# Weighted sums of gathered rows: from VectorE multiply-adds to TensorE products with diagonal matrices

## The chip, the cores and the metric

## The reference, cut to what matters

`x` has 2048 rows of 128 values. Four blocks follow each other, each added to `x` after a layer norm: a graph attention in hyperbolic space over a 2048x2048 mask, a linear layer computed in logarithms, a second graph attention, and a causal attention with 8 heads whose keys and values are looked up in a product-key memory. Only the last is touched:

```python
q = (x @ Wq).reshape(b, n, HEADS, DIM) * DIM ** (-0.5)
kv_scores, indices = _pk(x, Wq_pk, pk_keys)          # 16 best rows and their softmax weights
ind = indices + offsets[None, None, :, None]
k = jnp.einsum('bnhk,bnhkd->bnhd', kv_scores, keys_table[ind])
v = jnp.einsum('bnhk,bnhkd->bnhd', kv_scores, values_table[ind])
sim = jnp.einsum('bihd,bjhd->bhij', q, k)
...
attn = jax.nn.softmax(sim, axis=-1)
out = jnp.einsum('bhij,bjhd->bhid', attn, v)
```

For each of the 2048 positions and each head, 16 rows of 256 values (key and value side by side in one table) are fetched and summed with 16 weights. `_pk` finds the 16 best of 128x128 key pairs: the top 16 of each of two lists of 128 similarities, then the top 16 of the sums, of which 54 can qualify.

## The kernel before, in words

The positions are cut in T = 16 tiles of 128, one position per partition. Each engine has an instruction stream of its own, written out by hand, and the streams meet only at semaphores. The first 300 us or so hold the three earlier blocks. The last block then runs 8 heads x 16 tiles. Head 0 is written out, heads 1 to 6 are a hardware loop, head 7 is written out.

The gather (GpSimd, L281 to L291). For each tile GpSimd waits for the 16 row numbers of each position (`rows_full`) and for a free ring slot (`slot_free`), then issues 16 indirect DMAs, one for each k, each fetching 128 rows of 1 KB into `ring[:, t % 4, k, :]`. The ring has 4 slots, so the gathers run up to four tiles ahead. Semaphores `gathered[slot][quarter]` tell of each 4 landed DMAs; the last one of a head has `last_in`.

VectorE's step (L809 to L898). In step t it finds the row numbers of tile a = t + 4 (`find_start` to `find_best_second`, `find_best_index`, `look_up_1` to `look_up_5`), normalises the weights of tile t + 3 (`weigh_1`, `weigh_2`), takes the maximum over the scores of tile t - 1 (`score_max`), adds the finished output of tile t - 2 into `xs` (`add_out_1`, `add_out_2`), and, between all these, computes the 16 weighted sums of tile t: `sum_rows(t, k)` is acc = ring * weight + acc over 128x256, with `acc` in PSUM and the last one writing `kv[:, t, :]` (L749 to L755). The small operations are laid between the sums so that a result is never read by the next instruction. After the last sum the slot is given back (L882).

TensorE's step (L1639 to L1656). `project(t + 5)`: queries and the similarities with the product keys, with a wait for ScalarE between. `exponentials()`: wait for the softmax of tile t - 1. `values(t - 1)`: the probabilities are transposed in groups of four blocks, copied by ScalarE, multiplied with the values, then projected by `wo`. `turn_keys(t)`: wait for `kv_full`, transpose the new keys. `scores(t)`: q times all keys up to tile t, so that the work grows with t.

ScalarE's step (L1307 to L1322) holds the copies out of PSUM and the exponentials that go with these: `exp_best`, `project_out`, `softmax(t - 1)`, `turned_out(t - 1)`, `key_out(t)`.

The start of the last block overlaps with the end of the second graph attention: `masked(1, t)` on VectorE prepares its rows, and the searches for tiles 0 to 4 and the two halves of tile 0's sums (`sum_half`, L906) are laid between these and the closing ELU and normalisation of each group of tiles (`elu_in`, `elu_out`, `normal`, L957 to L971), which ScalarE (L1260 to L1267) and TensorE (L1549 to L1555) follow.

## Time and profile before

| | |
|---|---|
| runs | 2860.98, 2866.45, 2868.05 us; median 2866.45 |
| profiled execution | span 2859.2 us; the profile gives no other time of it |
| busy | PE 56%, PEld 43%, DVE 83%, ACT 26%, POOL 69% |
| DMA | 291.44 MB, mean 102 GB/s |
| mean granted TensorE clock | 0.702 |

The span runs from the first to the last instruction of the profiled execution, so it is a little shorter than a device time. PE is TensorE's matmuls, PEld its weight loads, DVE is VectorE, ACT ScalarE, POOL GpSimd. "DVEq", "PEq" and the like are the waits of an engine's instruction queue at a semaphore. Instructions that issue DMAs or handle semaphores aren't counted as busy, the generation of an indirect DMA's descriptors on GpSimd is.

### The profile page before, as it was taken

How to read it: one execution, taken by the hardware profiler on the slowest of the kernel's cores; microseconds unless marked ns; L12 is line 12 of the kernel's file. 1: busy time of each engine (PE TensorE's matmuls, PEld its weight loads, DVE VectorE, ACT ScalarE, POOL GpSimd, SP SyncE). 2: the span in 40 equal slices, each digit the busy share in tenths (PEclk: the TensorE clock that was granted, in tenths of full speed). 3: DMA queues.
4: the chain of work that ended last, by engine and by line, in shares of the span. 5: the costliest groups of instructions: out<-in, count | busy, mean ns of one | idle time of the engine just before them, and what ended most of it. 6: DMA issues, size and time to landing. Idle time of an engine off the chain costs nothing. (4 is left out here: it accounts for less than half of the span.)

```text
span 2859.2 us, 31735 instructions
## 1 busy us (share of the span) xinstructions
PE 1591.0 (56%) x7362; PEld 1220.4 (43%) x7362; DVE 2373.7 (83%) x8263; ACT 744.9 (26%) x1904; POOL 1959.6 (69%) x2064
## 2 busy tenths in 40 slices
PE   6858545664556445554556455554555445554555
PEld 6848434453344334442344234442344333442444
DVE  6689899998888888887888888887888888887874
ACT  5746412231122112221122112221122112221212
POOL 0003777777777777777777777777777777777775
PEclk8969756785578557775677557775678557775678
DMA  4201233333333333333333333333333333333333
GB/s 158 102 1 34 86 103 105 109 107 105 105 108 106 107 105 108 105 106 106 106 108 106 106 105 108 105 107 105 105 108 106 107 105 108 105 107 106 106 105 90
DMA packets 109551, 291.44 MB, mean 102 GB/s; under 512 B 34128, under 2 KB 41808, under 8 KB 107344
## 3 DMA queue, kind: packets, MB, share of 16 engines
q0 software_dynamic: 98304, 268.57, 32.1%
q1 hardware_dynamic: 10080, 20.97, 2.1%
q14 instruction: 127, 1.04, 0.1%
q8 instruction: 32, 0.52, 0.1%
q10 hardware_dynamic: 1008, 0.33, 0.0%
HBM read 288.69 MB, written 1.05 MB: 101 GB/s over the span
## 5 line engine op out<-in xcount | busy, mean ns | idle before, releaser
L288 POOL DMA_INDIRECT ring<-table,rows x2048 | 1952.1, 953 | 714.4 <-issue 587.9
L755 DVE SCALAR_TENSOR_TENSOR ps<-ring,wgt,ps 128x256 f32<-128x256 f32 x1792 | 865.6, 483 | 316.7 <-DMA ring<-table,rows 290.2
L1608 PE MATMUL ps<-ident,work 128*128 128x128 f32 x1088 | 260.2, 399 | 526.7 <-PEq L1601 526.7
L1608 PEld LDWEIGHTS ps<-ident,work 128*128 128x128 f32 x1088 | 201.4, 211 | 581.9 <-issue 581.8
L1622 PE MATMUL ps<-s2w,work 128*128 128x128 f32 x2176 | 418.7, 358 | 35.2 <-PEq L1620 34.4
L1622 PEld LDWEIGHTS ps<-s2w,work 128*128 128x128 f32 x2176 | 381.0, 265 | 84.5 <-issue 82.0
L1590 PE MATMUL ps<-work,qT 128*128 128x512 f32 (+3 forms) x576 | 310.7, 680 | 69.3 <-PEq L1582 64.8
L1296 ACT ACTIVATE s2w<-ps 128x512 f32<-128x512 f32 (+2 forms) x320 | 168.7, 533 | 332.2 <-ACTq L1295 331.8
L1286 ACT ACTIVATE work<-ps,nmax 128x128 f32<-128x128 f32 (+15 forms) x128 | 149.3, 1167 | 318.7 <-ACTq L1284 318.7
L1577 PE MATMUL ps<-ident,work 128*128 128x128 f32 x128 | 46.8, 366 | 316.9 <-PEq L1575 316.9
L1590 PEld LDWEIGHTS ps<-work,qT 128*128 128x128 f32 x576 | 124.9, 238 | 200.0 <-issue 200.0
L761 DVE TENSOR_REDUCE nmax<-ps 128x1 f32<-128x128 f32 (+7 forms) x127 | 160.8, 1266 | 10.8 <-DVEq L760 10.8
L1577 PEld LDWEIGHTS ps<-ident,work 128*128 128x128 f32 x128 | 20.8, 162 | 337.6 <-issue 337.2
L1274 ACT ACTIVATE qpk<-ps 128x128 f32<-128x128 f32 x123 | 34.1, 277 | 491.9 <-ACTq L1273 491.9
L1305 ACT ACTIVATE work<-ps 128x128 f32<-128x128 f32 x128 | 35.4, 277 | 457.1 <-ACTq L1304 457.0
L1571 PE MATMUL ps<-keyd,qpk 128*128 128x256 f32 x246 | 100.5, 496 | 90.3 <-PEq L1570 90.3
L1431 PE MATMUL ps<-work 128*128 128x128 f32 x1024 | 137.8, 280 | 2.8 <-PEq L1428 2.8
L727 DVE TENSOR_TENSOR pick<-bposf,ps 128x864 f32<-128x864 f32 x128 | 134.9, 1054 | 4.4
L731 DVE TENSOR_TENSOR pick<-pick,ps 128x864 f32<-128x864 f32 x128 | 134.9, 1054 | 4.4
L735 DVE TENSOR_REDUCE rowf<-pick 128x16 f32<-128x864 f32 x128 | 134.8, 1053 | 4.4
L1431 PEld LDWEIGHTS ps<-work 128*128 128x128 f32 x1024 | 127.1, 196 | 4.7 <-issue 4.5
L279 POOL TENSOR_TENSOR xs<-xs,bffn 128x512 f32<-128x512 f32 x4 | 5.9, 1477 | 162.6 <-DVE work L341 162.6
(241 smaller groups left out, 2654.3 us busy)
## 6 DMA issues: line engine op xcount, KB each, us to landing
ring<-table,rows POOLq DMA_INDIRECT x2048, 2.7
staged<-adj_in SPq DMA_DIRECT2D x16, 1024.0 KB, 4.8
xs<-x_in SPq DMA_DIRECT2D x4, 256.0 KB, 6.3
wpkq<-w_pkq SPq DMA_DIRECT2D x8, 128.0 KB
out<-xs SPq DMA_DIRECT2D x1, 832.0 KB, 4.4
keyd<-pk_keys SPq DMA_DIRECT2D x16, 32.0 KB
wo<-w_o SPq DMA_DIRECT2D x8, 64.0 KB
out<-xs SPq DMA_DIRECT2D x1, 192.0 KB, 2.1
```

Of the source, the lines that this page charges most:

```text
L288: nc.gpsimd.indirect_dma_start(ring[:, t % RING, k, :], None, table_d, bass.IndirectOffsetOnAxis(ap=rows[:, t % RING, k:k + 1], axis=0),). ...
L727: v.tensor_tensor(pick[:, :, :], bposf[:, :].unsqueeze(2).to_broadcast([P, TOPK, NCAND]), iota_ps.unsqueeze(1).to_broadcast([P, TOPK, NCAN ...
L731: v.tensor_tensor(pick[:, :, :], pick[:, :, :], cand_ps.unsqueeze(1).to_broadcast([P, TOPK, NCAND]), ALU.mult).then_inc(dve_done, c.one())
L735: v.tensor_reduce(rowf[:, :], pick[:, :, :], X, ALU.add).then_inc(dve_done, c.one())
L755: return v.scalar_tensor_tensor(out, row, w, acc_ps, ALU.mult, ALU.add)
L761: v.reduce_max(nmax[:, t % 2:t % 2 + 1], ps[:, 4:8, :].rearrange("p b n -> p (b n)")[:, 0:(t + 1) * P], X, negate=True).then_inc(nmax_full, 1)
L1286: s.activation(prob[:, t % 2, 0:L], ps[:, 4:8, :].rearrange("p b n -> p (b n)")[:, 0:L], ACT.Exp, bias=nmax[:, t % 2:t % 2 + 1], accum_out ...
L1296: s.activation(pts[:, (parity + b) % 2, 0:n * P], ps[:, 2 + (parity + b) % 2, 0:n * P], ACT.Copy).then_inc(pt_sb, 1)
L1431: ins = m.matmul(ps[:, OUT_BANKS[layer][t % banks], 0:D], ptg[:, n % 3, i * P:(i + 1) * P], hB[:, j, :], start=(j == 0), stop=(j == T - 1))
L1590: ins = m.matmul(ps[:, 4 + at // 512, 0:w], qT[:, t % 8, :], kT[:, at:at + w], start=True, stop=True)
L1608: ins = m.transpose(ps[:, 2 + (parity + b) % 2, j % 4 * P:(j % 4 + 1) * P], prob[:, t % 2, j * P:(j + 1) * P], ident[:, :])
L1622: ins = m.matmul(ps[:, 1, 0:P], kv[:, j, D:2 * D], pts[:, (parity + b) % 2, j % 4 * P:(j % 4 + 1) * P], start=(j == 0), stop=(j == t))
```

## The change

VectorE no longer sums. For each tile it makes one product, `spread(t)`: the 128x128 identity (a copy of it in PSUM) times each of the tile's 16 weights, 16 diagonal matrices side by side, 128x2048 elements, into one of two buffers that held rows of the graph attention. TensorE multiplies each diagonal matrix with the gathered rows of that k and accumulates the 16 products in PSUM (`sums`); ScalarE waits for that, gives the slot back, and copies the sum to `kv` (`kv_out`). The waits for landed rows move from VectorE to TensorE. The sums of tile t stand in TensorE's step ahead of the values of tile t - 1. In the last tile of the last head they are split around these. VectorE's step loses the interleaving; its parts follow each other with full fences (`drain`) between. The row numbers get 8 slots instead of 4. In the start, the search for tile 4 moves ahead of the ELU and normalisation of the last groups, and the sums of tile 0 are TensorE's and ScalarE's, ahead of their part of those groups.

```diff
-        rows = sb("rows", [P, RING, TOPK], U32)
+        rows = sb("rows", [P, ROWS, TOPK], U32)
...
+        kv_ps, end_ps = ps[:, 1, 2 * D:4 * D], ps[:, 0, 0:2 * D]
+        ident_ps = ps[:, 0, 3 * D:4 * D]
+        def diag(t):
+            return stagedf[:, 1 + t % 2, :].rearrange("p (k n) -> p k n", k=TOPK)
...
-            def sum_rows(t, k):
-
-                row, w = ring[:, t % RING, k, :], wgt[:, t % 4, k:k + 1]
-                if k == 0:
-                    return v.tensor_scalar(acc_ps, row, w, None, ALU.mult)
-                out = acc_ps if k < TOPK - 1 else kv[:, t, :] if t > 0 else acc[:, 0, :]
-                return v.scalar_tensor_tensor(out, row, w, acc_ps, ALU.mult, ALU.add)
+            def spread(t):
+
+                v.tensor_tensor(diag(t), ident_ps.unsqueeze(1).to_broadcast([P, TOPK, P]),
+                                wgt[:, t % 4, :].unsqueeze(2).to_broadcast([P, TOPK, P]), ALU.mult).then_inc(diag_ready, 1)
```

VectorE's step after the change:

```python
if find: find_start(a)
if out: add_out_1((t - 2) % T)
v.drain()
if find: find_replace(a)
if out: add_out_2((t - 2) % T)
v.drain()
if find: find_second(a)
if begun: score_max((t - 1) % T)
if not (last and t == T - 1): spread((t + 1) % T)
v.drain()
if find: find_index(a)
if weigh: weigh_1((t + AHEAD - 1) % T)
v.drain()
if weigh: weigh_2((t + AHEAD - 1) % T)
if find: find_all(a)
```

The start on VectorE, behind `find_all(3)`:

```diff
-            elu_out(3)
-            sum_half(0, 0)
-            normal(3)
-            elu_in(4)
-            weigh(2)
-            elu_out(4)
-            sum_half(0, 1)
-            normal(4)
-            rows_done(1)
-            find_halves(4)
-            find_all(4)
...
+            spread(0)
+            weigh(2)
+            find_halves(4)
+            elu_out(3)
+            find_all(4)
+            normal(3)
+            elu_in(4)
+            elu_out(4)
+            normal(4)
```

ScalarE and TensorE:

```diff
+            def kv_out(t, of=kv_ps):
+
+                act.wait_ge(sum_full, 1)
+                act.sem_inc(sum_full, -1)
+                act.sem_inc(slot_free, 1)
+                s.activation(kv[:, t, :], of, ACT.Copy).then_inc(kv_full, 1)
...
             query_out()
             sim_out(AHEAD)
+            kv_out(0)
...
+            def sums(h, t, quarters, to=kv_ps):
+
+                for q in quarters:
+                    if q == 0:
+                        pe.wait_ge(diag_ready, 1)
+                        pe.sem_inc(diag_ready, -1)
+                    landed(h, t, q)
+                    for k in range(q * QK, (q + 1) * QK):
+                        if t == T - 1 and k == TOPK - 1:
+                            pe.wait_ge(last_in, h * 16 + 16)
+                        ins = m.matmul(to, diag(t)[:, k, :], ring[:, t % RING, k, :], start=(k == 0), stop=(k == TOPK - 1))
+                    if q == QUARTERS - 1:
+                        ins.then_inc(sum_full, 1)
```

TensorE's step after the change, without its first step:

```python
project((t + AHEAD + 1) % T)          # not in the last head's last tiles
if last and t == T - 1:
    sums(h, t, (0,), end_ps)
    exponentials()
    past_scores(t).then_inc(s_full, 1)
    sums(h, t, (1, 2), end_ps)
    values(t - 1, PARITY[t - 1], bank1, t)      # quarter 3, key turn and own scores in its middle
    return
if t == 0:
    exponentials()
    values(T - 1, PARITY[T - 1], bank1)
    bank1()
    sums(h, 0, range(QUARTERS))
    kv_copied()
else:
    if t > 1:
        bank1()
    sums(h, t, range(QUARTERS))
    exponentials()
    values(t - 1, PARITY[t - 1], kv_copied)
turn_keys(t)
scores(t)
```

## Rows read from the trace of the kernel before

**Rows 1.** Page, first part: busy us (share of span) xinstructions.
```profile
PE 1591.0 (56%) x7362; PEld 1220.4 (43%) x7362; DVE 2373.7 (83%) x8263; ACT 744.9 (26%) x1904; POOL 1959.6 (69%) x2064
```

**Rows 2.** Line L288: ns min/median/max, first to last start; idle us, times.
```profile
L288 POOL DMA_INDIRECT ring<-table,rows x2048: 942/946/2361, 254.4 to 2836.4; - x187
...
  POOLq L286: 125.6, 115
```

**Rows 3.** GpSimd timeline: start us, us, operation, [idle before <-releaser].
```profile
308.93 1.14 POOL L288 DMA_INDIRECT ring<-table,rows  x1 [1.55 <-POOLq L286]
310.38 2.36 POOL L288 DMA_INDIRECT ring<-table,rows  x1 [0.30 <-issue]
...
357.33 0.94 POOL L288 DMA_INDIRECT ring<-table,rows  x1 [6.43 <-POOLq L286]
...
1401.19 0.95 POOL L288 DMA_INDIRECT ring<-table,rows  x1 [0.30 <-issue]
...
2836.43 0.95 POOL L288 DMA_INDIRECT ring<-table,rows  x1 [0.30 <-issue]
```

**Rows 4.** Groups by line, 600:2700: xcount | busy, mean ns | idle before.
```profile
L755 DVE SCALAR_TENSOR_TENSOR ps<-ring,wgt,ps 128x256 f32<-128x256 f32 x1482 | 715.1, 482 | 279.8 <-DMA ring<-table,rows 259.1
...
L727 DVE TENSOR_TENSOR pick<-bposf,ps 128x864 f32<-128x864 f32 x105 | 110.7, 1054 | 3.6
```

**Rows 5.** VectorE's timeline in the start, 300 to 357.
```profile
309.63 2.29 DVE L470 CUSTOM_DVE_ANT_0 staged<-staged,ring 128x2048 f32<-128x2048 f32 x1
...
326.78 0.40 DVE L738 CAST rows<-rowf 128x16 uint32<-128x16 f32 x1
...
334.18 0.16 DVE L565 TENSOR_TENSOR sc<-sc 128x4 f32<-128x4 f32 x1 [0.17 <-DVEq L310]
...
346.95 0.29 DVE L675 MAX8 half<-sim 128x8 f32<-128x128 f32 x1 [0.17 <-DVEq L673]
...
356.25 0.17 DVE L738 CAST rows<-rowf 128x16 uint32<-128x16 f32 x1
```

**Rows 6.** ScalarE's timeline in the start, 348 to 353.
```profile
348.86 0.38 ACT L1197 ACTIVATE aT<-ps 128x256 f32<-128x256 f32 x1 [1.08 <-ACTq L1196]
...
352.76 0.38 ACT L1280 ACTIVATE sim<-ps 128x256 f32<-128x256 f32 x1 [1.46 <-ACTq L1277]
```

**Rows 7.** TensorE timeline: an early light step, then a heavy one.
```profile
377.06 1.19 PE L1571 MATMUL ps<-keyd,qpk 128*128 128x256 f32 x2 [0.71 <-PEq L1570]
...
1565.08 3.46 PE L1590 MATMUL ps<-work,qT 128*128 128x512 f32 x8 [0.54 <-PEq L1582]
...
1578.02 1.94 PE L1608 MATMUL ps<-ident,work 128*128 128x128 f32 x8 [7.21 <-PEq L1601]
...
1586.18 0.46 PE L1637 MATMUL ps<-wo,oT 128*128 128x128 f32 x2 [0.54 <-PEq L1636]
...
1588.04 0.67 PE L1571 MATMUL ps<-keyd,qpk 128*128 128x256 f32 x2 [0.71 <-PEq L1570]
```

**Rows 8.** Windows: length, busy by engine, granted clock, DMA share, GB/s.
```profile
50.00:100.00 50.00, 50.00 (x442) 49.93 (x441) 40.48 (x66) 39.85 (x59) 0.00 (x0) 0.98 0.54 193
400.00:2780.00 2380.00, 1279.55 (x5169) 938.89 (x5170) 2011.69 (x7255) 512.02 (x1384) 1800.20 (x1904) 0.68 0.36 106
```

**Rows 9.** Timelines of VectorE, ScalarE and TensorE at the end, 2820 to 2843.
```profile
2820.85 0.48 DVE L755 SCALAR_TENSOR_TENSOR work<-ring,wgt,ps 128x256 f32<-128x256 f32 x1
2826.14 2.16 DVE L761 TENSOR_REDUCE nmax<-ps 128x1 f32<-128x1920 f32 x1 [4.82 <-DVEq L760]
...
2828.42 1.86 ACT L1286 ACTIVATE work<-ps,nmax 128x1920 f32<-128x1920 f32 x1 [6.25 <-ACTq L1284]
...
2830.52 5.16 PE L1590 MATMUL ps<-work,qT 128*128 128x512 f32 x8 [4.51 <-PEq L1601]
...
2836.97 2.02 PE L1622 MATMUL ps<-s2w,work 128*128 128x128 f32 x16 [0.43 <-PEq L1620]
...
2841.67 0.63 PE L1597 MATMUL ps<-work,qT 128*128 128x128 f32 x2
```

More of the change, by code:

```diff
@@ L675, in find_start @@
                 v.max(half[:, 0, 0, 0:8], sim[:, s, 0:NKEY])
-                v.max(half[:, 1, 0, 0:8], sim[:, s, NKEY:2 * NKEY]).then_inc(dve_done, c.one())
+                v.max(half[:, 1, 0, 0:8], sim[:, s, NKEY:2 * NKEY])
             def find_replace(t):
@@ L775, in add_out_2 @@
                                        ALU.mult, ALU.add).then_inc(bank1_free, 1)
-            def landed(h, t, q):
-                per = [16 * (QK - (q == QUARTERS - 1 and s == T - 1)) for s in range(t % RING, T, RING)]
-                dve.wait_ge(gathered[t % RING][q], h * sum(per) + sum(per[:t // RING + 1]))
-            def sum_even(t, k):
-                sum_rows(t, k).then_inc(dve_done, c.one())
-            def sum_odd(t, k):
-                settle()
-                sum_rows(t, k).then_inc(dve_done, c.one())
-                settle()
             def find_halves(t):
@@ L818, in step @@
                     find_start(a)
-                settle()
-                if last and t == T - 1:
-                    score_max(t - 1)
-                landed(h, t, 0)
-                sum_even(t, 0)
+                if out:
+                    add_out_1((t - 2) % T)
+                v.drain()
                 if find:
@@ L826, in step @@
                 if out:
-                    add_out_1((t - 2) % T)
-                if t == 1:
-                    v.tensor_copy(kv[:, 0, :], acc[:, 0, :]).then_inc(kv_full, 1)
-                sum_odd(t, 1)
-                sum_even(t, 2)
-                if out:
                     add_out_2((t - 2) % T)
+                v.drain()
                 if find:
                     find_second(a)
-                if prev and (t - 1) % T < 8:
+                if begun:
                     score_max((t - 1) % T)
-                sum_odd(t, 3)
@@ L840, in step @@
-                landed(h, t, 1)
-                sum_even(t, 4)
+                if not (last and t == T - 1):
+                    spread((t + 1) % T)
+                v.drain()
                 if find:
                     find_index(a)
-                if prev and (t - 1) % T >= 8 and not (last and t == T - 1):
-                    score_max((t - 1) % T)
-                sum_odd(t, 5)
-                sum_even(t, 6)
-                if find:
-                    find_rows(a)
                 if weigh:
@@ L882, in step @@
[L882 to L897 removed]
+                    find_all(a)
@@ L898, in step @@
+                if last and t == T - 1:
+                    v.drain()
                     dve.sem_inc(out_ready, 1)
@@ L904, in weigh @@
                 weigh_2(t)
-            def sum_half(t, part):
-                for k in range(8 * part, 8 * part + 8):
-                    if k % QK == 0:
-                        landed(0, t, k // QK)
-                    settle()
-                    sum_rows(t, k).then_inc(dve_done, c.one())
-                settle()
-                if part == 1:
-                    dve.sem_inc(slot_free, 1)
             dve.sem_inc(sim_free, 1)
@@ L1291, in turned_out @@
                     if key and b == 2:
+                        kv_out(key, end_ps)
                         key_out(key)
@@ L1317, in step @@
                     return
-                if not (first and t == 0):
-                    softmax((t - 1) % T)
-                    turned_out((t - 1) % T, PARITY[(t - 1) % T])
+                if first and t == 0:
+                    key_out(0)
+                    return
+                softmax((t - 1) % T)
                 if t > 0:
-                    key_out(t)
+                    kv_out(t)
+                turned_out((t - 1) % T, PARITY[(t - 1) % T])
+                if t == 0:
+                    kv_out(0)
+                key_out(t)
             for t in range(T):
@@ L1548, in _, with landed, bank1, kv_copied @@
             operands_ready()
+            def landed(h, t, q):
+                per = [16 * (QK - (q == QUARTERS - 1 and s == T - 1)) for s in range(t % RING, T, RING)]
+                pe.wait_ge(gathered[t % RING][q], h * sum(per) + sum(per[:t // RING + 1]))
+            def bank1():
+                pe.wait_ge(bank1_free, 1)
+                pe.sem_inc(bank1_free, -1)
+            def kv_copied():
+                pe.wait_ge(kv_full, 1)
+                pe.sem_inc(kv_full, -1)
+            def sums(h, t, quarters, to=kv_ps):
[10 more added lines that the diff above has]
+                        ins.then_inc(sum_full, 1)
             attend(1)
@@ L1551, in _ @@
             similar()
+            bank1()
+            sums(0, 0, range(QUARTERS))
             group(3)
@@ L1601, in exponentials, with values @@
                 pe.sem_inc(prob_full, -1)
-            def values(t, parity, key=None):
+            def values(t, parity, bank_free, key=None):
                 last = t // 4
@@ L1624, in values @@
                     if key and b == 1:
+                        sums(HEADS - 1, key, (QUARTERS - 1,), end_ps)
+                        kv_copied()
                         turn_keys(key)
```

143 lines of the change are left out of this document (48 added, 95 removed).

## The prediction, made before the changed kernel was run

> **What bounds the kernel now.** I read the page's busy shares first: VectorE 83%, GpSimd 69%, TensorE 56% [rows 1]. By that alone VectorE looks like the bound, and 1,792 of its instructions are the multiply-adds that this change takes away. The next view says otherwise. The one line of GpSimd that gathers table rows ran 2,048 times, from 254.4 to 2836.4 us, and waited at its semaphore for 125.6 us in all [rows 2]. Its timeline shows where: 83.5 us ahead of the first gather, 1.55 us ahead of gather 33, 6.43 us ahead of gather 65, and then never again more than the 0.30 us that each one has before it [rows 3]. In the steady part a gather is 0.95 us "busy" behind 0.30 us of issue (the one at 1401.19), so one starts each 1.25 us, and the missing 0.30 us is what makes the share look like 69%. From gather 65 at 357.33 to the last at 2836.43 there are 1,983 steps in 2479.1 us, 1.250 us each. So GpSimd issues without a break, and a tile costs 16 x 1.25 = 20.0 us whatever the others do. VectorE's own waits say the same: of the 279.8 us that it idled ahead of its sums between 600 and 2700, 259.1 were for landed rows [rows 4]. The pace is also 1.25 us in the last 57 us, where VectorE has little left to do, so a less busy VectorE doesn't quicken it. The time is then: start up to gather 65 (357.3) + 2479.1 + what follows the last gather (2859.2 - 2836.4 = 22.8). Only the first and the last term can move, unless some engine's work per tile passes 20.0 us.
>
> The profiled execution has a span of 2859.2 us; no time of its own is given beside it. The runs are 2860.98, 2866.45 and 2868.05, so the median is 7.3 us above the span. I work in the span and add 7.3.
>
> **The change, per tile in the steady part.**
> VectorE: out go 16 fused sums of 0.48 us [rows 4], 7.7 us. In comes one product over 128x2048. The trace has no such one; below, it can't be under the 1.05 us that 864 elements take [rows 4], above, three such products of 864 are 3.2 us. One VectorE pass over 128x2048 took 2.29 us [rows 5], and 1.05 x 2048/864 = 2.5; I take 2.3. Fences in place of counted waits cost some 0.04 us each, under 1 us a tile. VectorE falls from 2011.69/119 = 16.9 us a tile [rows 8] to some 12. Worth nothing: it wasn't the bound.
> TensorE: in come 16 products with 256 moving columns. At full clock 1,920 columns took 3.46 us [rows 7], so 256 take 0.43 to 0.46 (a single pair with its latency is 0.67) and 16 take 7.1; at half clock the single pair is 1.19 instead of 0.67 [rows 7], twice the columns' share, and 16 take 13.7 to 14. Weight loads hide, as they do now. TensorE has 1279.55/119 = 10.75 us a tile now, at a mean clock of 0.68 [rows 8]. The sum is 17.9 us with the new products at full clock, 24.8 at half clock; the limit is 20.0. This is the step that decides. In a heavy step: values 8.6 us (1578.02 to 1586.64), past scores 3.46 and 1.1 for key turn and own scores, projection 2.1 (to 1588.71) [rows 7], sums 7.1, together 22.4, of which some 2 come from the slow first microseconds after a 7.21 us idle [rows 7] that the new work would mostly fill. Light steps have some 13. Ring and row buffers let four tiles average out, so I take full or nearly full clock and no stall of GpSimd. Evidence for the clock: where TensorE was busy 50.00 of 50 us it was granted 0.98 [rows 8]; at 54% busy 0.68; and the burst at 1578 begins at half pace and ends at full.
> By the Trainium skill, "TensorE: Matmul & The Clock Gate", section "A second HAM failure mode: psum-queue depth-cycling", short idles between groups can keep the clock going up and down, so that dense-looking work still pays. That speaks against me, and the 0.5 us pauses ahead of many groups here are of that sort; it is rival 1.
> GpSimd: is it slowed by the new wide product? Gather 34 took 2.36 us [rows 3] while VectorE ran a 128x2048 pass with both inputs in SBUF [rows 5]. But the look-up products [rows 4], with one input in PSUM, run beside gathers whose median is 946 ns and least 942 [rows 2], and the new product has its identity in PSUM too. So nothing.
> The Trainium skill, "GPSIMD Engine Reference", section "Specifications", names as contending only VectorE instructions in a two-port mode or with two SBUF inputs; by that rule the sum stays as it is. If it fails here, each tile pays 2.36 - 0.95 = 1.4 us.
> ScalarE: a copy of 128x256, 0.38 us [rows 6], per tile, on an engine that is at 26%. Nothing.
>
> **The start.** GpSimd is through with the fourth tile at 357.33 - 6.43 = 350.9 and waits for the fifth tile's row numbers, written at 356.25 [rows 5]. Now their search is moved ahead. Row numbers of the fourth tile are done at 327.2 [rows 5] (later by 0.6 to 0.8 with the identity copy and the fences, which also move gather 33). Then product 2.3, weights 0.4 (330) and halves 3 (333); halves and search together take 9.5 now, from 346.95 to 356.4 [rows 5], and the search 6.5 of it. The ELU's second part needs an exponential of ScalarE, and a copy of tile 0's sums now stands ahead of it. TensorE can start these sums at 329.4 and needs 7.1 to 14 us; I take 9 (half pace at first): 338.5, copy and exponential to 339.8. ELU part 2.9, search 6.5: 349.3 (347 to 355). Gather 65 goes at 351.2 instead of 357.33: 6.1 us won.
> It is lost at gather 81. The normalisation chain that began at 334.18 [rows 5] now begins at 349.4. It ended at 349.24 [rows 6], 15.06 us later, with 3.8 us in it that were half of tile 0's sums; so now it ends at 360.7. The similarities of tile 5 follow 3.9 us later (349.24 to 353.14 [rows 6]), 364.3 here, and then halves 3.0, score maximum 0.3, product 2.3, weights and second index 1.0, search 6.5: 376.5 to 377.4. Its slot also needs tile 1's sums: first scores until 366, projection 2, sums 7.1 to 14: 375.5 to 382.5, likely 378. Gather 81 started at 357.33 + 20 = 377.33 and now starts at some 378.5 (377.4 to 383). So the start gives -0 to +5, I take +1.5.
>
> **The end.** Now the last-but-one tile's sums finish at 2821.33, its scores' maximum starts at 2826.14 and ends 2828.30, the softmax ends 2830.4 [rows 9]. The values of the tile before, 7.7 us, were done by TensorE while it waited for rows. In the new order TensorE sits in the sums and takes these values after them: the landing's chain is last quarter of sums 1.8, values 7, keys and scores 4.6, maximum 2.3, softmax 2.1, with 0.1 of waits 17.9. Its rows land 20 us ahead of the last tile's, at 2819.3, so 2837.2, against 2830.4. Then, all ahead of the last tile's own scores: past scores 3.5 (5.16 now, at half pace [rows 9]), two quarters of sums 3.6, half of the values 3.5 (2835.5 to 2839.0 now [rows 9]), the last quarter 1.9, ScalarE's copy 0.65, key turn and own scores 2.0: 15.2 together, 2852.4. That is 10.1 us after the 2842.30 at which own scores ended (2841.67 + 0.63 [rows 9]). Bounds: 9 with everything at full clock and overlapped, 20 with sums and values at half pace. From there to the end nothing changes, 17 us. The last rows land at 2839.6, so they are no longer what the end waits for. I take +10.5, for a wait or two more on the way.
>
> **Sum.** 2859.2 + 1.5 + 10.5 = 2871.2 span; + 7.3 = 2878.5, +0.4%.
>
> **Rivals.**
> 1. TensorE becomes the bound, at a clock that stays between. Against: it would be denser than now. For: 10.75 + 14 = 24.8 us at half clock, and in light steps a single pair takes 1.19 us, half pace [rows 7]. If a third of each head's tiles ran at half clock and the buffers took up half of their 4.8 us, 128/3 x 2.4 = +100 us: 2978; at one tile in eight +40 us, 2918. It decides once TensorE's mean passes 20.0 us, at an effective clock under some 0.85 for the sums. 0.14.
> 2. Not slower: the start keeps its 6.1 us because tile 1's sums are at full clock and the fifth search comes sooner than I chain it (VectorE's fences let ELU and search run closer), and the end costs its lower bound of 9. Then -(6.1 - 0.8) + 9 = +3.7: 2870. It decides where gather 81 starts before 374. 0.20.
> 3. The wide product slows the gathers: 128 x 1.4 = +180 us, 2878 + 180 = 3058. Against it stand the look-up products. 0.03.
> 4. It does what it says and the end is also cheaper, since TensorE is warm: 0 or less. A real gain over 0.3% would need more than the 8 us of waits in the start, with a free end: 2857. 0.04.
> The forecast has 0.59.
>
> **Range.** 0.3% of 2866 is 8.6 us, about what can be told from no change: 2857.9 and 2875.1 are the borders. Forecast's own range is 2870 to 2892 (start 0 to 5, end 9 to 20); about a fifth of its chance lies under 2875. Same: 0.59/5 + 0.20 = 0.32. Faster 0.04. Slower 0.64. The range to hold 8 in 10 reaches from rival 2 to the light form of rival 1: 2866 to 2912.
>
> **What would show it.** Right: gathers 1.25 us apart from gather 81 to the last, with no wait over 0.3; gather 65 near 351, gather 81 near 378; VectorE under 65% busy with no change in time; granted clock over 0.85 in the steady part; the last gather near 2838 and 33 us from there to the end instead of 22.8. Wrong: waits of GpSimd for its slots (ScalarE's release after the sums) in the heads, gathers over 0.95 us beside the new product, or a granted clock of 0.5 beside full sums.

## The result: 0.4% slower, and the profile after

The changed kernel takes 2878.88 us (median of 4 runs, 2873.7 to 2882.34). The kernel before, timed beside it on the same chip, takes 2867.16 us (median of 4, 2860.98 to 2868.05). The ratio is 1.0042, with a 95% interval of 1.003 to 1.0053: slower, by 11.7 us. The profiled execution of the changed kernel has a span of 2871.8 us, against 2859.2 before, so the spans differ by 12.6 us and can be used to split the loss. Both profiled executions are 5 to 6 us quicker than their medians, so they are compared with each other and not with these. Every ratio here compares runs of one state, without those more than 1.5% above the fastest of the same kernel, so on some chips it differs from the quotient of the medians beside it.

The code moved by seven lines at the gather: L288 of before is L295 after, its wait L286 is L293. L758 is the new wide product, L1504 are the new products on TensorE, L1141 is ScalarE's copy of the sums.

The page's busy shares and TensorE's granted clock in 40 slices, to be held against [rows 1]:

```profile
PE 2220.4 (77%) x11458; PEld 1784.0 (62%) x11458; DVE 1865.3 (65%) x6336; ACT 779.9 (27%) x2032; POOL 1960.1 (68%) x2064
...
PEclk9969889999899989999999889999999899999999
```

TensorE went from 1591.0 to 2220.4 us busy, VectorE from 2373.7 to 1865.3. 508 us of VectorE's work are gone, and the kernel is not faster. GpSimd's figure is the one that did not move: 1959.6 and 1960.1 us. The gather's line shows the same (ns least/median/most, first to last start, then its waits), to be held against [rows 2]:

```profile
L295 POOL DMA_INDIRECT ring<-table,rows x2048: 940/946/2421, 255.3 to 2839.7; - x187
...
  POOLq L293: 127.3, 109
...
DMA to landing us min/median/max: 2.6/2.8/4.6
```

The same stretch of the steady part as in [rows 8] (length, busy time of PE, PEld, DVE, ACT, POOL, clock, DMA share, GB/s), and the two new groups:

```profile
400.00:2780.00 2380.00, 1868.08 (x9046) 1465.42 (x9044) 1537.72 (x5443) 544.36 (x1506) 1800.05 (x1905) 0.94 0.37 107
```

```profile
L1504 PE MATMUL ps<-ring,staged 128*128 128x256 f32 x4096 | 1019.7, 406 | 229.3 <-DMA ring<-table,rows 209.8
...
L758 DVE TENSOR_TENSOR staged<-ps,wgt 128x2048 f32<-128x2048 f32 x128 | 291.9, 2281 | 0.2 <-issue 0.2
```

Over 119 tiles TensorE has 1868.08/119 = 15.7 us a tile and VectorE 12.9, both under the 20.0 us that GpSimd takes for 16 gathers. The granted clock rose from 0.68 to 0.94. The new products waited 209.8 us for landed rows: TensorE, like VectorE before it, waits for GpSimd. GpSimd's timeline (start us, us, idle before) gives the three parts of the time, to be held against [rows 3]:

```profile
310.53 1.17 POOL L295 DMA_INDIRECT ring<-table,rows  x1 [1.57 <-POOLq L293]
...
352.71 1.03 POOL L295 DMA_INDIRECT ring<-table,rows  x1 [0.30 <-issue]
...
380.93 0.94 POOL L295 DMA_INDIRECT ring<-table,rows  x1 [8.29 <-POOLq L293]
...
2839.72 0.94 POOL L295 DMA_INDIRECT ring<-table,rows  x1 [0.30 <-issue]
```

Gather 65, at 352.71, no longer waits; gather 81 at 380.93 waits 8.29 us, and it did not wait before. From there the 1,967 steps to the last gather take 2458.8 us, 1.250 us each. So the last gather starts at 2839.72 instead of 2836.43, 3.3 us later, and from it to the end of the span are 32.1 us instead of 22.8, 9.3 us more. The two make the 12.6 us.

**The start.** VectorE, ScalarE and TensorE, for [rows 5 to 7]:

```profile
329.03 0.17 DVE L745 CAST rows<-rowf 128x16 uint32<-128x16 f32 x1
329.18 2.29 DVE L758 TENSOR_TENSOR staged<-ps,wgt 128x2048 f32<-128x2048 f32 x1
...
341.42 0.69 DVE L555 SCALAR_TENSOR_TENSOR fin<-fin,work 128x512 f32<-128x512 f32 x1 [6.61 <-DVEq L317]
...
344.27 0.17 DVE L701 CAST half<-pos 128x16 f32<-128x16 uint32 x1
...
350.96 0.20 DVE L745 CAST rows<-rowf 128x16 uint32<-128x16 f32 x1
...
378.71 0.17 DVE L745 CAST rows<-rowf 128x16 uint32<-128x16 f32 x1
```

```profile
340.38 0.38 ACT L1141 ACTIVATE work<-ps 128x256 f32<-128x256 f32 x1 [11.97 <-ACTq L1139]
340.65 0.62 ACT L940 ACTIVATE fin<-fin 128x512 f32<-128x512 f32 x1
...
380.19 0.38 ACT L1141 ACTIVATE work<-ps 128x256 f32<-128x256 f32 x1 [8.69 <-ACTq L1139]
```

```profile
331.61 8.57 PE L1504 MATMUL ps<-ring,staged 128*128 128x256 f32 x32 [3.89 <-PEq L1499]
...
370.44 9.56 PE L1504 MATMUL ps<-ring,staged 128*128 128x256 f32 x32
...
385.07 0.67 PE L1532 MATMUL ps<-keyd,qpk 128*128 128x256 f32 x2 [0.71 <-PEq L1531]
...
400.10 7.07 PE L1504 MATMUL ps<-ring,staged 128*128 128x256 f32 x32
```

The wide product took 2.29 us. TensorE began tile 0's sums after 3.89 us of idleness and took 8.57 us for them, ScalarE's copy stood in its queue from 328.4 until 340.38, and the exponential for the ELU behind it. So the ELU's second part waited 6.61 us of VectorE's time, and the fifth tile's row numbers came at 350.96 to 351.16 instead of 356.42. Gather 81 had its row numbers at 378.88 (the last of VectorE's rows) and then needed the slot of tile 1, whose sums ended at 380.00 after 9.56 us, begun at half pace (the last row shows the same 32 instructions at full clock: 7.07), and whose copy (the one at 380.19) released it.

**The end.** TensorE, with the maximum of the last-but-one tile's scores on VectorE and its softmax on ScalarE, for [rows 9]:

```profile
2822.48 3.47 PE L1504 MATMUL ps<-ring,staged 128*128 128x256 f32 x8 [2.46 <-DMA ring<-table,rows]
...
2836.66 1.89 PE L1504 MATMUL ps<-ring,staged 128*128 128x256 f32 x8
2841.34 3.46 PE L1549 MATMUL ps<-work,qT 128*128 128x512 f32 x8 [2.79 <-PEq L1560]
2844.64 3.62 PE L1504 MATMUL ps<-ring,staged 128*128 128x256 f32 x16
...
2851.41 1.89 PE L1504 MATMUL ps<-ring,staged 128*128 128x256 f32 x8
...
2855.16 0.39 PE L1556 MATMUL ps<-work,qT 128*128 128x128 f32 x2
```

```profile
2836.97 2.16 DVE L765 TENSOR_REDUCE nmax<-ps 128x1 f32<-128x1920 f32 x1 [3.75 <-DVEq L764]
```

```profile
2839.25 1.86 ACT L1214 ACTIVATE work<-ps,nmax 128x1920 f32<-128x1920 f32 x1 [6.26 <-ACTq L1212]
```

The last quarter of that tile's sums ran near half pace (3.47 us for its 8 instructions, against 1.89 for the 8 at 2836.66), then came the earlier tile's values, and the maximum started at 2836.97 where it had started at 2826.14. TensorE idled for 2.79 us until the softmax had ended; only then came past scores, two quarters of the last tile's sums, half of the values and the last quarter, one after another. The last tile's own scores ended at 2855.55, against 2842.30 before.

### The profile page after: what moved, and what is told of

The parts are those of the page before. It is cut to its first block and busy times, and to the rows that moved or that the text cites. A ratio compares the mean times of both kernels' runs of the same rounds, so it can differ in the third digit from the quotient of the medians.

```text
span 2871.8 us, 39679 instructions
## 1 busy us (share of the span) xinstructions
PE 2220.4 (77%) x11458; PEld 1784.0 (62%) x11458; DVE 1865.3 (65%) x6336; ACT 779.9 (27%) x2032; POOL 1960.1 (68%) x2064
## 3 DMA queue, kind: packets, MB, share of 16 engines
HBM read 288.69 MB, written 1.05 MB: 101 GB/s over the span
## 5 line engine op out<-in xcount | busy, mean ns | idle before, releaser
L295 POOL DMA_INDIRECT ring<-table,rows x2048 | 1952.6, 953 | 717.9 <-issue 586.0
L1504 PE MATMUL ps<-ring,staged 128*128 128x256 f32 x4096 | 1019.7, 406 | 229.3 <-DMA ring<-table,rows 209.8
L1504 PEld LDWEIGHTS ps<-ring,staged 128*128 128x128 f32 x4096 | 813.1, 202 | 404.6 <-DMA ring<-table,rows 263.0
L1141 ACT ACTIVATE work<-ps 128x256 f32<-128x256 f32 x128 | 49.0, 383 | 1054.0 <-ACTq L1139 1054.0
L1580 PE MATMUL ps<-s2w,work 128*128 128x128 f32 x2176 | 307.9, 289 | 34.0 <-PEq L1578 33.1
L1580 PEld LDWEIGHTS ps<-s2w,work 128*128 128x128 f32 x2176 | 276.0, 200 | 65.7 <-issue 62.6
L1549 PE MATMUL ps<-work,qT 128*128 128x512 f32 (+3 forms) x576 | 244.2, 554 | 67.6 <-PEq L1541 64.8
L758 DVE TENSOR_TENSOR staged<-ps,wgt 128x2048 f32<-128x2048 f32 x128 | 291.9, 2281 | 0.2 <-issue 0.2
L1567 PE MATMUL ps<-ident,work 128*128 128x128 f32 x1088 | 194.1, 304 | 39.9 <-PEq L1560 21.0
L1549 PEld LDWEIGHTS ps<-work,qT 128*128 128x128 f32 x576 | 102.1, 194 | 174.1 <-issue 174.1
L1567 PEld LDWEIGHTS ps<-ident,work 128*128 128x128 f32 x1088 | 148.6, 159 | 78.9 <-issue 67.4
```

Of the source, the lines that this page charges most:

```text
L295: nc.gpsimd.indirect_dma_start(ring[:, t % RING, k, :], None, table_d, bass.IndirectOffsetOnAxis(ap=rows[:, t % ROWS, k:k + 1], axis=0),). ...
L758: v.tensor_tensor(diag(t), ident_ps.unsqueeze(1).to_broadcast([P, TOPK, P]), wgt[:, t % 4, :].unsqueeze(2).to_broadcast([P, TOPK, P]), ALU ...
L1504: ins = m.matmul(to, diag(t)[:, k, :], ring[:, t % RING, k, :], start=(k == 0), stop=(k == TOPK - 1))
L1549: ins = m.matmul(ps[:, 4 + at // 512, 0:w], qT[:, t % 8, :], kT[:, at:at + w], start=True, stop=True)
L1567: ins = m.transpose(ps[:, 2 + (parity + b) % 2, j % 4 * P:(j % 4 + 1) * P], prob[:, t % 2, j * P:(j + 1) * P], ident[:, :])
L1580: ins = m.matmul(ps[:, 1, 0:P], kv[:, j, D:2 * D], pts[:, (parity + b) % 2, j % 4 * P:(j % 4 + 1) * P], start=(j == 0), stop=(j == t))
```

## The experiments

They ran on three chips. On one the kernel before took 2864 to 2866 us, about as in the prediction's runs (2866.45). On the other two it took about 3.9 ms, and the profiles taken there show many waits ahead of instructions for nothing that the profile names; those chips are told last. The changed kernel itself was not run again on the first of these three, so "11.7 us over" below is its distance to the kernel before on its own chip.

**1. Was VectorE worth anything?** The kernel before, with 14 of its 16 weighted sums of each tile on 32 columns instead of 256.

```diff
+                if k < TOPK - 1:
+                    return v.scalar_tensor_tensor(acc_ps[:, 0:32], row[:, 0:32], w, acc_ps[:, 0:32], ALU.mult, ALU.add)
```

> The kernel before with 14 of VectorE's 16 sums per tile over 32 columns instead of 256; the other columns of these sums are left out. VectorE loses some 14 x 0.3 = 4.2 us a tile. My theory (GpSimd's pace is the bound, VectorE's sums cost nothing): the same time, ratio 0.998 to 1.000, gathers still each 1.25 us. Rival (VectorE at 83% is the bound, or its work slows GpSimd): 3 to 20% faster.

Measured: 2858.89 us (2858.24 to 2859.9, 10 runs), ratio 0.9983 (0.9974 to 0.9992).

```profile
400.00:2780.00 2380.00, 1280.01 (x5162) 936.96 (x5163) 1596.49 (x7214) 510.14 (x1378) 1800.42 (x1903) 0.68 0.37 106
```

VectorE lost 415 us of work in this stretch, 3.5 us a tile, and GpSimd did the same as before to 0.2 us. The profiled execution is 2.6 us shorter than that of the kernel before: 2.7 us are won in the start (gather 81 at 374.65 instead of 377.33), 1.5 in the end (21.3 us after the last gather at 2835.28, instead of 22.8), and 1.5 are lost between these two gathers (2460.6 us instead of 2459.1). By the ratio it is 4.9 us; where the other 2 lie was not followed. So a fifth of VectorE's work is worth a few microseconds at the ends, and between gather 81 and the last nothing is won.

**2. Does the wide product slow the gathers?** The change, with the identity read from SBUF in place of PSUM; nothing else.

```diff
-                v.tensor_tensor(diag(t), ident_ps.unsqueeze(1).to_broadcast([P, TOPK, P]),
+                v.tensor_tensor(diag(t), ident[:, :].unsqueeze(1).to_broadcast([P, TOPK, P]),
```

> The changed kernel with the identity of the wide product read from SBUF instead of PSUM, so both inputs are in SBUF. My theory of the neighbour rule (such a pass holds up the gather beside it, as 2.36 us beside a 128x2048 pass in the start): one or two gathers of each tile take up to 1.4 us longer, +130 to +200 us, ratio 1.05 to 1.07. Rival (the start's long gathers have another cause): no gather over 1.0 us after gather 81, same time as the changed kernel.

Measured: 3073.9 us (3071.57 to 3079.38, 4 runs), ratio 1.073 (1.0713 to 1.0746). The timeline of this kernel, and under it that of the changed kernel at the same work:

```profile
1501.13 2.28 DVE L758 TENSOR_TENSOR staged<-ident,wgt 128x2048 f32<-128x2048 f32 x1
...
1501.62 2.62 POOL L295 DMA_INDIRECT ring<-table,rows  x1 [0.31 <-issue]
...
1521.88 2.28 DVE L758 TENSOR_TENSOR staged<-ident,wgt 128x2048 f32<-128x2048 f32 x1
...
1522.07 2.91 POOL L295 DMA_INDIRECT ring<-table,rows  x1 [0.30 <-issue]
```

```profile
1516.23 2.28 DVE L758 TENSOR_TENSOR staged<-ps,wgt 128x2048 f32<-128x2048 f32 x1
...
1517.24 0.95 POOL L295 DMA_INDIRECT ring<-table,rows  x1 [0.30 <-issue]
```

The VectorE pass is 2.28 us in both. With two inputs in SBUF the gather beside it takes 2.62 and 2.91 us and ends 0.8 us after the pass; with the identity in PSUM the gather takes its 0.95 us in the middle of the pass. It is so all along: behind gather 81 there are 125 such passes, each holds up one gather, which then takes 1.9 to 3.0 us and ends 0.81 to 0.84 us after the pass. Together they take 199 us more than at 0.95 us each, and from gather 81 to the last are 2659.7 us instead of 2458.8, 201 more; nothing else is needed to explain the loss. In the changed kernel no gather behind gather 81 takes over 1.0 us. The ratios of the two kernels differ by 0.0688, 197 us, or 1.5 us for each of the 128 tiles, at the upper end of the 130 to 200 us expected; the ratio, 1.073, is just over the 1.05 to 1.07. So rival 3 of the prediction was a real danger with the right price (1.4 us a tile), and what avoids it is one operand's place.

**3. The start: one copy in ScalarE's order.** The change, with ScalarE's copy of tile 0's sums moved behind the exponential that VectorE's ELU part waits for.

```diff
-            kv_out(0)
             for g in (3, 4):
                 elu_exp(g)
+                if g == 3:
+                    kv_out(0)
```

> The moved copy in the start once more (ScalarE copies tile 0's sums after ELU group 3's exponential), on a chip where instructions don't wait to be issued, since on the first chip each tile lost several us of that kind in both kernels and the start couldn't be told. My theory: gather 81 at 374.5 to 376 instead of 380.9, span 5 to 6.5 us under the changed kernel's 2871.8, so ratio to the kernel before 1.0015 to 1.003. Rival (ring slot of gather 81 held by tile 1's sums whatever the copy does): ratio as the changed kernel's, 1.003 to 1.005.

Measured: 2870.98 us (2869.23 to 2873.23, 11 runs), ratio 1.0024 (1.0014 to 1.0033).

```profile
335.43 0.69 DVE L555 SCALAR_TENSOR_TENSOR fin<-fin,work 128x512 f32<-128x512 f32 x1 [0.18 <-DVEq L317]
```

```profile
353.67 0.95 POOL L295 DMA_INDIRECT ring<-table,rows  x1 [0.30 <-issue]
...
374.81 0.95 POOL L295 DMA_INDIRECT ring<-table,rows  x1 [1.43 <-POOLq L293]
```

The ELU part waits 0.18 us instead of 6.61 and gather 81 goes at 374.81 instead of 380.93, as expected. It still waits for the slot of tile 1, but tile 1's sums hang on the same chain and came sooner too, so the rival is out. The kernel is 7.0 us over before instead of 11.7: 4.7 us won by the ratios, a little under the 5 to 6.5 expected, and as the ratios' intervals (up to 1.0033 and from 1.003) just touch, the size is rough. Of the two profiled executions this one is only 2.7 us shorter: 6.1 us are won at gather 81, 2.2 lost from there to the last gather (2461.0 us instead of 2458.8) and 1.2 behind it, where past scores ran at half pace (5.13 us instead of 3.46):

```profile
2836.99 5.13 PE L1550 MATMUL ps<-work,qT 128*128 128x512 f32 x8 [2.79 <-PEq L1561]
```

**4. The end: more of the sums ahead of the wait.** The same, and in the last tile TensorE does three quarters of its sums, not one, before it waits for the softmax.

```diff
-                    sums(h, t, (0,), end_ps)
+                    sums(h, t, (0, 1, 2), end_ps)
                     exponentials()
                     past_scores(t).then_inc(s_full, 1)
-                    sums(h, t, (1, 2), end_ps)
```

> The moved copy and the two quarters of sums ahead of the softmax's wait in the last tile. My theory: start and end are separate terms, 5 to 6.5 and 2.5 to 3 us: 7.5 to 9.5 us under the changed kernel, 2.5 to 3 us under the run with the moved copy alone, ratio to the kernel before 1.000 to 1.002. Rival (the end waits for the last landed rows): no difference to the moved copy alone.

Measured: 2866.61 us (2862.37 to 2868.37, 11 runs), ratio 1.001 (1.0 to 1.0019): the kernel before's time, as near as can be told. Gather 81 and the last gather, and TensorE behind that (its lines stand one higher here):

```profile
373.95 0.95 POOL L295 DMA_INDIRECT ring<-table,rows  x1 [0.68 <-issue]
...
2833.01 0.94 POOL L295 DMA_INDIRECT ring<-table,rows  x1 [0.30 <-issue]
```

```profile
2815.84 1.99 PE L1505 MATMUL ps<-ring,staged 128*128 128x256 f32 x8 [2.60 <-DMA ring<-table,rows]
...
2828.33 5.35 PE L1505 MATMUL ps<-ring,staged 128*128 128x256 f32 x24
2833.51 3.38 PE L1550 MATMUL ps<-work,qT 128*128 128x512 f32 x8
...
2843.81 0.39 PE L1557 MATMUL ps<-work,qT 128*128 128x128 f32 x2
```

TensorE goes from sums to past scores without the 2.79 us of idleness. Own scores end at 2844.20, 11.2 us after the last gather; in the changed kernel it was 15.8, in the one before 5.9. Of these 4.6 us, 3.0 are the order's: from the start of the last tile's sums to the own scores' end are 15.9 us (2828.33 to 2844.20), in the changed kernel 18.9 (2836.66 to 2855.55). That is the 2.5 to 3 expected. The other 1.6 lie ahead of the edit, where tile 14's last quarter ran near full clock here (1.99 us, not 3.47). The medians put it at 4.4 us over experiment 3, more than expected; why is not shown, since the profiled execution is the quickest of its eleven and already 2.8 us ahead of that of experiment 3 at the last gather. Each set against the kernel before on its own chip, the change is 11.7 us over and this version 2.6: both orders together bring 9.1 us, and 7.5 to 9.5 were expected.

**5. Is it TensorE's or VectorE's turn once GpSimd has less to do?** The change with 12 gathers a tile; the other four rows aren't fetched, and a neighbour's row stands in for each row that is not gathered, so that all 16 products are still made (the semaphores' counts follow).

```diff
                 for k in range(TOPK):
+                    if k % QK == QK - 1:
+                        continue
...
-                        ins = m.matmul(to, diag(t)[:, k, :], ring[:, t % RING, k, :], ...)
+                        ins = m.matmul(to, diag(t)[:, k, :], ring[:, t % RING, k - (k % QK == QK - 1), :], ...)
```

> The changed kernel with 12 gathers per tile and still 16 products on TensorE, once more, since on the last chip all engines waited for their own instructions and the run told nothing. The row left out is replaced by its neighbour. My theory: GpSimd's share falls to 15 us a tile and TensorE becomes the bound at 16.6 us a tile on the mean, 2440 to 2500 us, under what the kernel before could reach with as few gathers: its VectorE alone has 16.9 us of work a tile, 357 + 124 x 16.9 + 23 = 2476 without any wait. Rival (TensorE's clock falls or its chain of waits stretches): over 2500 us.

Measured: 2538.1 us (2537.03 to 2539.5, 4 runs), ratio 0.8855 (0.884 to 0.887). The expectation is missed by 38 us. After the steady stretch, the new products' line on the page; then four of GpSimd's gathers.

```profile
400.00:2450.00 2050.00, 1739.53 (x9021) 1410.68 (x9020) 1533.02 (x5439) 543.26 (x1504) 1375.16 (x1452) 0.98 0.33 95
```

```profile
L1506 PE MATMUL ps<-ring,staged 128*128 128x256 f32 x4096 | 924.2, 384 | 19.2 <-PEq L1501 19.2
```

```profile
380.89 0.94 POOL L297 DMA_INDIRECT ring<-table,rows  x1 [14.12 <-POOLq L293]
...
644.11 0.94 POOL L297 DMA_INDIRECT ring<-table,rows  x1 [18.75 <-POOLq L293]
...
2281.79 0.94 POOL L297 DMA_INDIRECT ring<-table,rows  x1 [19.07 <-POOLq L293]
...
2460.95 0.94 POOL L297 DMA_INDIRECT ring<-table,rows  x1 [0.30 <-issue]
```

Now TensorE is the bound: its new products no longer wait for landed rows (209.8 us in the changed kernel, none here), and GpSimd waits for slots instead. From 644.11 to 2281.79 there are 96 tiles, 17.06 us each, against 15.0 for GpSimd's 12 gathers. The clock is 0.98, so not a falling clock. TensorE is busy for 1739.53 of the 2050 us, 14.4 of 17 us a tile; the rest is idle.

The expectation went wrong in two places. It took the pace at 16.6 us; the sum behind it (2871.8 - 124 x 3.3, in the expectation for the same kernel under 6) takes off 3.3 us a tile. The measured pace takes off 2.9, and over 124 tiles that alone lifts the span from 2463 us to some 2507. The other 30 us are an end that it left out: TensorE is behind GpSimd by then, and 77 us follow the last gather (2537.7 less 2460.95) where the changed kernel has 32. So the time is the rival's, over 2500, and of the rival's two reasons the clock is out; whether waits within TensorE's step make the difference in pace was not followed.

It shows that the 16 gathers are what holds the changed kernel at 20.0 us a tile: a quarter of them taken away is worth 11% against the kernel before, where a fifth of VectorE's work was worth 0.2%. With the gathers the bytes fell too, so one may ask whether the DMA engines set the 1.25 us rather than GpSimd's issue. The traces speak against it: rows land 2.6 to 4.6 us after their issue, the DMA engines are busy for a share of 0.37, and the first gather after a wait of 14 or 19 us, with all earlier ones landed, takes the same 0.94 us as any other. No run changed the bytes alone.

**6. The chips on which instructions come late.** The changed kernel, experiments 3 and 4, and the end's edit alone ran on one of them first.

> The changed kernel again, beside the next three on one chip. My theory: GpSimd's gathers, one each 1.25 us, are the bound in both kernels, so the difference to the kernel before is start + end: gather 81 some 3.6 us later (380.9 against 377.3) and 9 us more from the last gather to the end (32 against 22.8). Expected ratio 1.0035 to 1.005, +10 to +14 us. Rival (TensorE's new load stalls the gathers in the heads): GpSimd would show waits after gather 81; expected none by my theory.

> One line moved on ScalarE: the copy of tile 0's sums comes after the exponential of ELU group 3 instead of ahead of it. My theory: VectorE waited 6.6 us there (for an exponential queued behind TensorE's 8.6 us of sums), and all of the start's loss hangs on it. Expected: VectorE's ELU part starts at some 335 instead of 341.4, gather 81 at 374.5 to 376 instead of 380.9, the time 5 to 6.5 us lower than the changed kernel's. Rival (gather 81 is held by its ring slot, by tile 1's sums at half pace, which the swap doesn't move): gather 81 stays at 380 to 381 and the time is the same.

> One edit on TensorE in the last tile of the last head: quarters 1 and 2 of its sums go ahead of the wait for the softmax of tile 14 instead of behind it. My theory: the end is a chain on TensorE, and the 3.6 us of these two quarters stand on it while TensorE idles 2.8 us ahead of them. Expected: past scores of tile 15 start 0 to 1 us later, own scores end 2.5 to 3 us earlier, time 2.5 to 3 us lower. Rival (the end waits for the last rows to land): nothing moves, within 0.5 us.

> Both edits. If start and end are separate terms on either side of a stretch that GpSimd alone sets, the gains add: 7.5 to 9.5 us lower than the changed kernel, so within 3 to 5 us of the kernel before, ratio 1.000 to 1.002. Rival (some stage in the heads swallows an earlier start): only the end's 2.5 to 3 us are left.

Measured, beside 3920.92 us of the kernel before (3883 to 4022, 11 runs): the changed kernel 3775.55 us, ratio 0.9618 (0.9566 to 0.967); the start's edit 3765.86, 0.9592 (0.9538 to 0.9646); the end's edit 3762.45, 0.9588 (0.9534 to 0.9643); both 3762.36, 0.9586 (0.952 to 0.9652). The four can't be told apart, so the single microseconds that these expectations speak of can't be judged there, and the ratios near 1 were missed: all four are 4% faster than the kernel before. VectorE in the changed kernel there, then the wait of the gather's line, then ScalarE's copy:

```profile
1511.15 0.22 DVE L724 MAX8 best<-candr 128x8 f32<-128x54 f32 x1 [2.35 <-issue]
...
1514.64 0.17 DVE L731 CAST bposf<-bpos 128x8 f32<-128x8 uint32 x1 [2.43 <-issue]
```

```profile
  POOLq L293: 978.3, 127
```

```profile
1518.47 0.38 ACT L1141 ACTIVATE work<-ps 128x256 f32<-128x256 f32 x1 [12.86 <-ACTq L1139]
```

VectorE waited 2.35 and 2.43 us ahead of single short instructions for nothing that the profile shows; 309.1 us in all ahead of the one line, 196.7 ahead of the other. The copy that frees a slot started at 1518.47, though TensorE had ended these sums 8 us earlier, at 1510.60. So GpSimd waited 978.3 us for slots, and its gathers were no slower (median 949 ns). Here the change does pay. It has 1,927 fewer instructions on VectorE; whether that is the reason was not tested, and the kernel before was not profiled on this chip.

On the other such chip ran three more. The kernel before with 12 gathers, each sum of a row not fetched taking its neighbour (the semaphores' counts follow, and the wait for a head's last row moves ahead of the sum that now needs it):

```diff
+                    if k % QK == QK - 1:
+                        continue
...
-                row, w = ring[:, t % RING, k, :], wgt[:, t % 4, k:k + 1]
+                row, w = ring[:, t % RING, k - (k % QK == QK - 1), :], wgt[:, t % 4, k:k + 1]
```

> The kernel before with 12 gathers per tile instead of 16; each fourth row is left out, its product takes the row ahead of it, so VectorE still makes 16 sums. GpSimd's own time falls to 15 us a tile. My theory: now VectorE's 16.9 us of work a tile is the bound, with small waits some 17.3 us, so 124 tiles give back 2.7 us each: a span of 2510 to 2560. Rival (each gather's landing or the DMA engines set the 20 us, not GpSimd's issue): the time falls by a quarter of the 2480 us, to some 2240.

The change with 12 gathers, as in experiment 5:

> The changed kernel with the same 12 gathers, still 16 products on TensorE. My theory: TensorE becomes the bound, at 12.3 + 0.57 t us of a step at full clock, 16.6 on the mean, so 2871.8 - 124 x 3.3 = 2460, 2440 to 2500; the change is then worth 2 to 4% instead of costing 0.4%. Rival (TensorE's clock falls as soon as it leads): no faster than the kernel before with 12 gathers.

And a version with five edits: those of experiments 3 and 4, the identity's copy moved behind the first searches, counted waits instead of fences in the second half of the start's searches, and, in the last-but-one tile, the earlier tile's values between the halves of its sums.

```diff
-            find_all(0)
+            find_all(0, True)
...
+                if last and t == T - 2:
+                    pe.wait_ge(diag_ready, 2)
+                    bank1()
+                    sums(h, t, (0, 1), end_ps)
+                    exponentials()
+                    values(t - 1, PARITY[t - 1], lambda: None)
+                    sums(h, t, (2, 3), end_ps)
```

> The changed kernel with five edits: the moved copy; quarters 0 to 2 of the last tile's sums ahead of the softmax's wait; the identity's copy into PSUM behind the first searches instead of in them; counted waits instead of fences in the start's searches; in tile 14 of the last head the values of tile 13 between the two halves of its sums, which go to bank 0. My theory: against the run with the first two, the row numbers of the third tile come 1.6 us sooner, of which 0.8 to 1.6 reach gather 81, and the end is 2 to 2.5 us shorter: 3 to 4 us under it, ratio to the kernel before 0.9990 to 1.0002. Rival (gather 81 then waits for its slot or its row numbers just as long): only the end's 2 us.

Measured, beside 3913.6 us (3853 to 3976, 11 runs): 3099.7, ratio 0.7995 (0.7925 to 0.8064), for before with 12 gathers; 3169.86, 0.8152 (0.8065 to 0.824), for the change with 12; 3769.67, 0.9715 (0.9639 to 0.9791), for the five edits. All three expectations are missed as they stand (2510 to 2560 and 2440 to 2500 us, and a ratio of 0.999 to 1.0002). None was made for such a chip, so their reasons can't be judged by it, and as the kernel before scatters by 3% there, these ratios are rough. Between the two kernels with 12 gathers no run overlaps (3094 to 3103 and 3147 to 3190 us): the change is behind by 2%, while with 16 it is ahead by 4% on the other chip. Whether the change is the better kernel on a quiet chip once GpSimd has less to do stays open: VectorE's 16.9 us a tile before and TensorE's 17.0 in experiment 5 are too near to say. Whether the five edits beat the kernel before on a quiet chip stays open too. No version with all the work in it did.

## Why the prediction came out right, by its own steps

**The bound.** Right, and it is the step that made the rest. GpSimd's 1.25 us a gather held from gather 81 to the last, 1,967 steps, with 508 us less on VectorE and 629 us more on TensorE (result), and with VectorE lightened alone (experiment 1). The mistake to be avoided was the busy share: 83% was not a bound, 69% was. One reason given for it was weaker than it sounds: in the last 57 us VectorE was not idle but half busy (31 of the 60 us from 2780 to 2840). Experiment 1 settles what that was meant to show.

**Steady part.** The product was put at 2.3 us (2.28 measured), 16 products at 7.1 (7.07 in a row at full clock; 1019.7/128 = 8.0 on average), VectorE at some 12 us a tile (12.9; where the 0.9 lies was not followed), TensorE at 17.9 (15.7: beside 8.0 for the sums the old work took 7.7 instead of 10.75, since the higher clock shortened it too, which the sum left out: 10.75 x 0.68/0.94 = 7.8). The clock was said to rise over 0.85, and was 0.94. Rival 1 needed TensorE's mean to pass 20 us.

**The start** was mis-sized: +1.5 predicted, +3.3 measured. The searches with fences took 6.9 us (344.27 to 351.16) where 6.5 were taken, and the identity's copy came ahead; gather 33 was 1.6 us late (310.53 less 308.93), where 0.6 to 0.8 had been allowed. And the forecast names these 0.6 to 0.8 us but starts TensorE's sums at 329.4, which is 327.2 + 2.3 without them; they started at 331.61, behind row numbers that were there at 329.20. Gather 65 was predicted at 351.2 and went at 352.71; gather 81 at 378.5 (377.4 to 383) and went at 380.93. The mechanism, that what is won at gather 65 is lost at gather 81 because a copy on ScalarE holds the exponential, was right: experiment 3 puts the copy behind the exponential and gather 81 goes at 374.81.

**The end** was mis-sized the other way: +10.5 predicted, +9.3 measured from the last gather on. The 10.1 us to the own scores' end came to 9.95 besides the shift of 3.3 (2855.55 less 2842.30 less 3.3), and the 0.4 added for a wait or two never came. The remaining tail was 0.65 us shorter (16.25 us from own scores to the end of the span, 16.9 before): TensorE's seven transposes right behind the own scores took 0.93 us at 2855.39, and 1.70 at 2842.09 before, where it ran at half pace. That past scores and sums in a row are what it costs, and not the landing, is shown by experiment 4, where the order alone takes 3.0 us out of this stretch while the last rows land as before.

So of the sum's +12.0 us, 12.6 measured, the start's error of +1.8 and the end's of -1.2 offset each other. The forecast was nearer than its parts, and that is luck. So is the last step: the 7.3 us from span to median were carried over, and came to 7.1 (2878.88 less 2871.8). In the changed kernel only 1.9 of these lie between span and time of one execution (2873.7 less 2871.8); the rest is how far the profiled execution lies under the median, and nothing says that it should be alike for both kernels.

Some sums in the prediction are slightly off, and none decides. 360.7 + 3.9 is 364.6 and not 364.3; first scores until 366, projection 2 and sums of 7.1 to 14 give 375.1 to 382 and not 375.5 to 382.5; and the forecast's own range, given as from 2870, begins at 2875.5 by its own bounds (2859.2 + 0 + 9 + 7.3). The measured 2878.88 lies in it either way.

**The rivals.** TensorE as the bound: no, with 4.3 us a tile to spare. Not slower than before: no as it stood, since gather 81 went at 380.93 and not before 374; but with the two orders of experiments 3 and 4 its condition is met, gather 81 at 373.95, and the ratio is 1.001; the end's edit has its part in that. The wide product slowing gathers: no, and experiment 2 shows that it is the identity's place in PSUM that spares them. Faster through a free end: no.

## What to carry to other kernels

Find the engine whose instructions follow each other at one pace over the whole span, by the first and the last start of its line and the waits between; its busy share can be far under that of an engine that only fills its waits. Work taken from another engine then is worth what it does in the start and the end, and there the order of an in-order queue counts: a copy that waits for a new step must not stand ahead of one that others need, and what can be done before a wait should be. Before a wide VectorE pass is put beside gathers that GpSimd issues, look where its operands lie.

## What the hardware showed that was not expected

A gather beside a VectorE pass over 128x2048 with both inputs in SBUF takes 1.9 to 3.0 us instead of 0.95, to 0.8 us past the pass's end, one gather for each of 125 passes, and the pass itself is not slowed (2281 ns in both kernels). With one input in PSUM nothing is seen, in 128 such passes of the changed kernel. The Trainium skill, "GPSIMD Engine Reference", section "Specifications", names VectorE instructions with two SBUF inputs as ones that contend; the trace agrees, and puts the whole cost on GpSimd, 199 us in the profiled execution.

TensorE's granted clock was 0.68 in the kernel before, busy for 1279.55 of 2380 us, 0.94 in the changed one, busy for 1868.08, and 0.98 in experiment 5, busy for 1739.53 of 2050. The Trainium skill, "TensorE: Matmul & The Clock Gate", section "A second HAM failure mode: psum-queue depth-cycling", warns of short idles between groups; pauses like the 0.71 us ahead of the row at 385.07 are still there after the change, and the granted clock was high all the same. No run set pauses alone against none.

One program, the kernel before, took 2.87 ms on one chip and 3.9 on two others. The changed kernel's profile there has "issue" waits of over 2 us ahead of 0.2 us instructions, and a change that loses 0.4% on the one gains 4% on the other. Where a profile shows such waits, a result is one of that chip, and is not carried over to another.
